# Fourteen blocks of the first feed-forward matrix quantised during attention, diagonal tiles regrouped, low-rank closers issued by four

## The chip, the cores and the metric

The kernel runs on the 8 cores of one Trainium2 chip. Each core computes one of the 8 sequences of the batch; the weights are the same for all, and the cores exchange nothing. The metric is the device time in microseconds of the slowest core.

## What is computed

```
x = layernorm(x + attention(x) @ W_O)              # 2048 tokens, 1024 features, 16 heads of 64 + 32 rotary
    Q = [cq @ W_UQ, rope(cq @ W_QR)], K = [ckv @ W_UK, rope(x @ W_KR)], V = ckv @ W_UV
    scores = clip(Q K^T, -80, 80), causal, softmax(scores / sqrt(96)) @ V
x = layernorm(x + W_proj'(gelu(W_fc' x)))           # 1024 -> 4096 -> 1024
    W' x = fake_quant(W) x + b + 2 * B (A x)        # low-rank adapter of rank 16
    fake_quant(W): s = max|W| / 127;  round(W / s) clipped to [-128, 127], times s
```

The scale s is one number for each matrix, so the whole matrix must have been read once before any of it can be rounded.

## The kernel before

All five engines run programs written out by hand, with semaphores between them; each engine does its work in the order in which the program lists it. Four stretches follow one another.

**Inputs.** Up to about 91 us the latent projections, the values (into the tile VP, all in bf16) and the first pair of heads are made.

**Attention.** Heads go in 8 pairs (NPAIR). A pair has 36 units (NU), numbered g = 0 to 287 over the pairs. A unit is one tile of 128 keys against a block of 512 queries, for both heads of the pair. In a query block the three tiles past the first diagonal one (kt = 4 qb + 1, + 2, + 3, of 384, 256 and 128 columns) share two units. For each unit TensorE writes scores into one of two PSUM slots (PSD0, PSD1; `scores`, L551), ScalarE takes the exponential into one of eight tiles PT0 to PT7 (L802), VectorE clips it (L1036 on the diagonal, L1040 elsewhere), and five units later (LAG) TensorE multiplies by the values (L582) and by ones for the denominators (L588). `released` holds back the scores of item j until the slot of item j - 2 was read. Four "next" items in each pair make the queries and keys of the next pair (L563), copied out by ScalarE (L810) and VectorE (L1022). A "scale" item spreads the quantisation scales to all partitions.

Beside this both feed-forward matrices are read once, 64 blocks of 512 KB, and VectorE takes the maximum of one block every fourth unit (`absmax`, L946, up to g = 253). The scales follow at g = 262 and 266, and from g = 274 VectorE rounds 7 pieces (`round_piece`, L881).

**Output projection and first layer norm.** TensorE does 32 steps s, each 8 matmuls with W_O (L659) and two sums over the features (`sums`, L632, L635). VectorE adds the residual (L1064), subtracts the mean (`centred`, L996) and multiplies by the inverse deviation (`normal`, L1001). ScalarE makes a copy and a square (L834, L835). The first matrix is quantised in these steps: ScalarE adds the magic number that rounds (L820), VectorE subtracts it and writes bf16 (`integers`, L889). Pieces are numbered k = 0 to 63, of which 0 to 31 are the first matrix (RTF) and 32 to 63 the second (RTP). SyncE loads them (L437) into 15 buffers (STG, QX and, when their tokens are normalised, the residual tiles XR).

**Feed-forward.** Eight chunks t of 256 tokens. `up(t, oc)` makes block oc of 32: 8 matmuls with RTF (L703) and a closer (L711), the low-rank part, which for t = 0 has 16 rows and for later t 128 rows, most of them zero. UPB gives five PSUM banks in turn. ScalarE applies gelu (L856). `down(t, dc)` is 32 matmuls with RTP (L724), then the adapter (L729), and `statistics` of the second layer norm (L679, L682), which need the sum that VectorE makes (L1136). In chunk 0 VectorE still quantises: `quant_upto(dc)` says up to which piece before the sum of block dc.

## Time and profile before

| | |
|---|---|
| three runs | 1077.07, 1077.62 and 1115.05 us, median 1077.62 |
| profiled execution | 1077.04 us, span of its slowest core (core 6) 1075.4 us |
| spans of the eight cores | 1071.1 to 1075.4 us |
| TensorE busy | 976.9 us, 91% of the span |
| ScalarE busy | 658.0 us, 61% |
| VectorE busy | 546.3 us, 51% |
| GpSimd busy | 60.1 us, 6% |

The span reaches from the first to the last instruction of a core. A busy share is a mean over all stretches: ScalarE and VectorE work hardest in attention, and little in the feed-forward part. Engine times of matmuls are modelled and may overlap by a little. The run of 1115.05 us lies apart from the other two, which are within 0.05%.

### The profile page before, as it was taken

What the parts mean: (1) busy time and instruction counts of PE and PEld (TensorE: products, weight loads), DVE (VectorE), ACT (ScalarE), POOL (GpSimd) and SP (SyncE); (2) the same over time, 40 slices, a digit from 0 to 9 for tenths busy, and PEclk for the clock granted to TensorE, in tenths of its full rate; (3) what the DMA queues carried; (4) which work ended last, traced back from release to release, by engine and by line L of the source; (5) the groups of instructions that cost most, each with busy time, mean ns of one, the idle gap of its engine ahead of it and who ended that gap; (6) DMA issues with size and microseconds to landing.
All of it is one profiled execution on the core that took longest, in us unless ns stands there. A gap on an engine that the chain in (4) does not pass through costs nothing.

```text
span 1075.4 us, 23227 instructions; the slowest of 8 cores (1071.1 to 1075.4 us)
## 1 busy us (share of the span) xinstructions
PE 976.9 (91%) x8227; PEld 668.5 (62%) x8242; DVE 546.3 (51%) x1059; ACT 658.0 (61%) x954; POOL 60.1 (6%) x113
## 2 busy tenths in 40 slices
PE   4998888888898888997789999999999999999995
PEld 1343444444444444443356788888888888888884
DVE  4457787887878877779895403112031120402114
...
GB/s 132 176 85 41 117 109 127 100 128 99 148 145 131 128 71 279 223 259 219 170 183 208 68 1 18 24 7 35 2 26 16 16 26 1 41 1 21 21 12 69
DMA packets 35439, 99.05 MB, mean 92 GB/s; under 512 B 4544, under 2 KB 12992, under 8 KB 34944
## 3 DMA queue, kind: packets, MB, share of 16 engines
...
## 4 chain that ended last, share of the span: by engine, by line
PE 66%; ACT 10%; DVE 10%; issue 8%; DMA 5%; POOL 1%; DVEq 0%; ACTq 0%; SPq 0%; POOLq 0%
PE PSD L703 17%; PE PS L724 15%; PE PSD L551 8%; ACT PT L802 7%; PE PSD L724 5%; PE PS L703 4%; DMA WUK<-wUK 4%; DVE QK L1022 2%; PE PSD L711 2%; PE PSD L563 2%; ACT RD L770 2%; PE BIG L582 2%; PE BIG L588 2%; DVE XA L1001 1%; PE PS L582 1%
## 5 line engine op out<-in xcount | busy, mean ns | idle before, releaser
L802 ACT ACTIVATE PT<-PSD 128x1024 bf16<-128x1024 f32 (+1 forms) x288 | 271.4, 979 | 21.8 <-PE PSD L551 20.0
L703 PE MATMUL PSD<-XA,RTF 128*128 128x256 bf16 x1664 | 212.8, 276 | 5.4 <-ACT HH L856 3.1
L551 PE MATMUL PSD<-QK 96*64 96x512 bf16 (+7 forms) x1280 | 175.9, 356 | 33.3 <-ACT PT L802 18.6
L703 PEld LDWEIGHTS PSD<-XA,RTF 128*128 128x128 bf16 x1664 | 162.2, 99 | 28.7 <-issue 6.7
L724 PE MATMUL PS<-HH,RTP 128*128 128x256 bf16 x1536 | 176.6, 274 | 0.0
L856 ACT ACTIVATE HH<-PSD,BFCS,SML 128x256 bf16<-128x256 f32 x208 | 115.0, 564 | 81.2 <-PE PSD L711 80.8
L724 PEld LDWEIGHTS PS<-HH,RTP 128*128 128x128 bf16 x1536 | 149.8, 98 | 19.8 <-issue 1.7
L551 PEld LDWEIGHTS PSD<-QK 96*64 96x64 bf16 (+1 forms) x1280 | 63.5, 109 | 125.4 <-issue 114.8
L1040 DVE TENSOR_SCALAR PT<-PT 128x1024 bf16<-128x1024 bf16 (+3 forms) x288 | 108.4, 381 | 42.0 <-ACT PT L802 39.7
L1125 DVE TENSOR_SCALAR UPt<-PSD,SML 128x256 bf16<-128x256 f32 x8 | 3.9, 484 | 234.2 <-PE PSD L743 234.2
L1136 DVE TENSOR_TENSOR XA<-PTMP,XA 128x256 bf16<-128x256 f32 x64 | 27.2, 425 | 143.8 <-ACT PTMP L865 143.6
L865 ACT ACTIVATE PTMP<-PS,BPRS,SML 128x256 f32<-128x256 f32 x48 | 26.9, 561 | 111.8 <-PE PS L729 111.8
L946 DVE TENSOR_REDUCE MXW<-STG 128x1 f32<-128x1024 f32 x64 | 77.7, 1214 | 0.0
L582 PE MATMUL BIG<-PT,VP 128*64 128x512 bf16 (+3 forms) x384 | 70.0, 351 | 4.1 <-DVE XA L952 3.7
L588 PE MATMUL BIG<-PT,ONES 128*64 128x512 bf16 (+3 forms) x384 | 70.1, 351 | 0.0
L659 PE MATMUL PSD<-XA,WOB 128*128 128x512 bf16 x249 | 59.6, 379 | 0.5 <-issue 0.2
L871 ACT ACTIVATE TSQ<-XA 128x256 bf16<-128x256 bf16 x64 | 26.7, 417 | 54.3 <-DVE XA L1136 54.3
L724 PE MATMUL PSD<-HH,RTP 128*128 128x256 bf16 x512 | 58.5, 273 | 0.0
L1036 DVE SCALAR_TENSOR_TENSOR PT<-PT,TRI 128x256 bf16<-128x256 bf16 (+1 forms) x96 | 48.9, 510 | 15.4 <-ACT PT L802 14.7
L724 PEld LDWEIGHTS PSD<-HH,RTP 128*128 128x128 bf16 x512 | 50.1, 98 | 5.8
L703 PE MATMUL PS<-XA,RTF 128*128 128x256 bf16 x384 | 49.8, 273 | 0.0
L711 PE MATMUL PSD<-UZ,BSF 128*128 128x256 bf16 x182 | 49.6, 273 | 0.0
...
## 6 DMA issues: line engine op xcount, KB each, us to landing
STG<-wFCr POOLq DMA_DIRECT2D x32, 512.0 KB, 3.9
STG<-wPRr POOLq DMA_DIRECT2D x32, 512.0 KB, 4.1
STG<-wPRr SPq DMA_DIRECT2D x24, 512.0 KB, 5.1
STG<-wFCr SPq DMA_DIRECT2D x20, 512.0 KB, 8.6
XR<-xP POOLq DMA_DIRECT2D x16, 512.0 KB, 8.6
...
QX<-wFCr SPq DMA_DIRECT2D x12, 512.0 KB, 8.7
XR<-wPRr SPq DMA_DIRECT2D x8, 512.0 KB, 7.6
```

Of the source, the lines that this page charges most:

```text
L551: mm = e.matmul(PSD[slot][64 * hf:64 * hf + 64, 512 * i + at:512 * i + at + ext], KH[c % 2][i][0:rows, 128 * kt + 64 * hf:128 * kt + 64 * ...
L582: e.matmul(OB[n % 2][64 * i:64 * i + 64, lq:lq + ext], VP[:, o:o + 64], PTB[g % NPT][:, 512 * i + at:512 * i + at + ext], start=first, sto ...
L588: mm = e.matmul(DB[n % 2][64 * i:64 * i + 64, lq:lq + ext], ONES[:, :], PTB[g % NPT][:, 512 * i + at:512 * i + at + ext], start=first, sto ...
L659: mm = e.matmul(BK[s % 4][:, 0:512], WOB[:, 1024 * ds + 128 * hc:1024 * ds + 128 * hc + 128], xa(hc, 512 * nb, 512), start=(hc == 0), stop ...
L703: e.matmul(UPB[oc % 5][:, 0:TC], RTF[:, 1024 * oc + 128 * i:1024 * oc + 128 * i + 128], xa(i, TC * t, TC), start=(i == 0), stop=False)
L711: e.matmul(UPB[oc % 5][:, 0:TC], lhs, rhs, start=False, stop=True).then_inc(s_fc, 1)
L724: e.matmul(DNB[dc % 3][:, 0:TC], RTP[dc][:, 128 * f:128 * f + 128], HH[:, TC * f:TC * f + TC], start=(f == 0), stop=False)
L802: e.activation(heads2(PTB[a % NPT], 0, ext), heads2(PSD[j % 2], 0, ext), AF.Exp, scale=ISQ).then_inc(s_exp, 1)
L856: e.activation(HH[:, TC * oc:TC * oc + TC], UPB[oc % 5][:, 0:TC], AF.Gelu, bias=BFCS[:, oc:oc + 1], scale=SML[:, 2:3]).then_inc(s_gelu, 1)
L946: e.tensor_reduce(MXW[:, ci:ci + 1], STG[:, 1024 * (ci % 4):1024 * (ci % 4) + 1024], AXX, ALU.max, apply_absolute_value=True).then_inc(s_a ...
L1036: e.scalar_tensor_tensor(heads2(pt, 0, lo), heads2(pt, 0, lo), LO, TRI[:, 0:2 * lo].rearrange("p (h x) -> p h x", h=2), ALU.max, ALU.min). ...
L1040: e.tensor_scalar(heads2(pt, lo, ext), heads2(pt, lo, ext), HI, LO, ALU.min, ALU.max).then_inc(s_clip, 1)
```

## The change

1. 14 pieces (EARLY) are quantised during attention. Piece k is rounded by VectorE at unit g = 181 + 7k and subtracted at g = 184 + 7k, so up to g = 275. They pass through the three QX buffers. Their output is written into blocks 8 to 21 of RTF (BLOCKS), which is where the values VP lie. VP is laid out by pairs of heads now, 2048 columns a pair, so that a pair's values are free when its attention is done: `integers(k)` waits for s_pv = 36 (k // 2 + 1).
2. The two scales are no longer made together. The maximum of the first matrix is taken at g = 132 and its scale at g = 140, with a second "scale" item behind unit 148.
3. SyncE issues the loads of pieces 0 to 6 behind the queries of pair 6 (when the scores of 180 units are done) and of 7 to 13 behind those of pair 7.
4. In the output projection ScalarE's rounding and VectorE's subtraction are in steps 3 to 20 and 4 to 21 as before, but VectorE has none in steps 15, 16 and 17 and none after 21. ScalarE's last two pieces, behind the last deviation, are gone. VectorE rounds pieces 36 to 45 itself. `quant_upto` is 58 + 3 dc in place of 56 + 3 dc, and there are 19 buffers, four of them in XR0.
5. The units of the diagonal are 384 and 128 + 256 columns in place of 128 + 384 and 256.
6. For chunk 0 the closers of four blocks stand together behind the fourth block, each with 32 rows in a strip of its own.

```diff
@@ pair_units
-        units += [(qb, [4 * qb + 3, 4 * qb + 1]), (qb, [4 * qb + 2])]
+        units += [(qb, [4 * qb + 1]), (qb, [4 * qb + 3, 4 * qb + 2])]
...
-SCALE_AT = NG - 26
+SCALE_AT = (140, NG - 26)
...
+    EARLY, EARLY_AT = 14, 181
+    BLOCKS = list(range(8, 22)) + list(range(8)) + list(range(22, 32))
...
-    BUF = [k % 7 for k in range(32)] + [7, 8, 9, 10, 0, 1, 2, 3, 11, 12, 13, 14] + \
-        [k % 4 for k in range(44, NK)]
+    BUF = [4 + k % 3 for k in range(EARLY)] + [k % 7 for k in range(EARLY, 32)] + \
+        [0, 1, 2, 3, 0, 1, 9, 10, 2, 3, 11, 12, 13, 14, 0, 1, 2, 3, 15, 16, 17, 18] + \
+        [k % 4 for k in range(54, NK)]
+    RESIDUAL = {9: 16, 11: 24, 15: 32}
-    ON_SCALAR = range(7, 38)
+    ON_SCALAR = range(21, 36)
...
-        return min(NK, 56 + 3 * dc)
+        return min(NK, 58 + 3 * dc)
@@ sp
         for c in range(1, NPAIR - 1):
             e.wait_ge(s_qk, NU * c)
             rotary(c + 1)
+            if c == 3:
+                maximum(0)
+            if c == 5:
+                for k in range(7):
+                    fetch(k)
+        for k in range(7, EARLY):
+            fetch(k)
+        maximum(1)
@@ pe, attend
-                    o = D * kt + 64 * (2 * c + i)
+                    o = 2048 * c + 128 * kt + 64 * i
@@ pe, up
-            else:
-                rows = slice(32 * r, 32 * r + 16)
-                lhs, rhs = BSF[rows, 128 * q:128 * q + 128], UO[rows, o:o + TC]
-            e.matmul(UPB[oc % 5][:, 0:TC], lhs, rhs, start=False, stop=True).then_inc(s_fc, 1)
+            elif r == 3:
+                for j in range(4):
+                    rows = slice(32 * j, 32 * j + 32)
+                    e.matmul(UPB[(oc - 3 + j) % 5][:, 0:TC], BSF[rows, 128 * q:128 * q + 128],
+                             UO[rows, 0:TC], start=False, stop=True).then_inc(s_fc, 1)
@@ act
-            if s >= 3:
-                round_piece(s + 4)
+            if 3 <= s < 14:
+                round_piece(s + 18)
+            elif 17 <= s < 21:
+                round_piece(s + 15)
         deviation(3)
-        round_piece(36)
-        round_piece(37)
@@ dve
+            k = (g - EARLY_AT) // 7
+            if 0 <= k < EARLY and (g - EARLY_AT) % 7 == 0:
+                if k == 0:
+                    e.wait_ge(s_sml, 1)
+                round_piece(k)
+            if 0 <= k < EARLY and (g - EARLY_AT) % 7 == 3:
+                e.wait_ge(s_pv, NU * (k // 2 + 1))
+                integers(k)
...
-            elif s >= 4:
-                integers(s + 3)
+            elif 4 <= s < 15:
+                integers(s + 17)
+            elif 18 <= s < 22:
+                integers(s + 14)
...
-        integers(35)
         for md in (6, 7):
             normal(2, md)
         moments(3)
-        integers(36)
-        for k in range(38, 45):
+        round_piece(36)
+        for k in range(37, 46):
             quant_step(k)
```

VectorE in attention, units 180 (PT4) to 184 (PT0) before. L1036 and L1040 clip, L946 is the maximum, L1022 copies out the keys and queries of the next pair:

```order
L1036 SCALAR_TENSOR_TENSOR PT4_66<-PT4_66,TRI_74 128x2x128
L1040 TENSOR_SCALAR PT4_66<-PT4_66 128x2x384
L1036 SCALAR_TENSOR_TENSOR PT5_67<-PT5_67,TRI_74 128x2x256
L1040 TENSOR_SCALAR PT5_67<-PT5_67 128x2x256
L946 TENSOR_REDUCE MXW_126<-STG_72 128x1
L1036 SCALAR_TENSOR_TENSOR PT6_68<-PT6_68,TRI_74 128x2x128
L1040 TENSOR_SCALAR PT6_68<-PT6_68 128x2x128
L1040 TENSOR_SCALAR PT7_69<-PT7_69 128x1024
L1040 TENSOR_SCALAR PT0_62<-PT0_62 128x1024
L1022 CAST QK0_59<-PSD0 64x2x512
```

The same stretch in the changed kernel, where L1066, L1070, L975 and L1051 are those lines, L910 rounds and L918 subtracts:

```order
L1066 SCALAR_TENSOR_TENSOR PT4_66<-PT4_66,TRI_74 128x2x128
L1070 TENSOR_SCALAR PT4_66<-PT4_66 128x2x384
L1066 SCALAR_TENSOR_TENSOR PT5_67<-PT5_67,TRI_74 128x2x128
L1070 TENSOR_SCALAR PT5_67<-PT5_67 128x2x256
L975 TENSOR_REDUCE MXW_126<-STG_72 128x1
L910 TENSOR_SCALAR QX0_76<-QX0_76,SML_130 128x1024
L1066 SCALAR_TENSOR_TENSOR PT6_68<-PT6_68,TRI_74 128x2x256
L1070 TENSOR_SCALAR PT6_68<-PT6_68 128x2x128
L1070 TENSOR_SCALAR PT7_69<-PT7_69 128x1024
L1070 TENSOR_SCALAR PT0_62<-PT0_62 128x1024
L918 TENSOR_SCALAR RTF_86<-QX0_76 128x1024
L1051 CAST QK0_59<-PSD1 64x2x512
```

Piece 0 is rounded behind unit 181's maximum and subtracted just ahead of the copy for the next pair; the two diagonal units have changed shapes.

VectorE in the output projection, steps 15, 16 and 17 before (L1064 adds, L996 subtracts the mean, L889 subtracts the magic number, L1001 normalises, L984 begins the moments of the second quarter):

```order
L1064 TENSOR_TENSOR XR1_80<-PSD1,XR1_80 128x512
L996 TENSOR_TENSOR XR0_79<-XR0_79,PS4 128x512 x2
L889 TENSOR_SCALAR RTF_86<-QX0_76 128x1024
L1001 TENSOR_TENSOR XA_43<-XR0_79,RSC0_99 128x512 x2
L1064 TENSOR_TENSOR XR2_81<-PSD0,XR2_81 128x512
L996 TENSOR_TENSOR XR0_79<-XR0_79,PS4 128x512 x2
L889 TENSOR_SCALAR RTF_86<-QX1_77 128x1024
L1001 TENSOR_TENSOR XA_43<-XR0_79,RSC0_99 128x512 x2
L1064 TENSOR_TENSOR XR2_81<-PSD0,XR2_81 128x512
L889 TENSOR_SCALAR RTF_86<-QX2_78 128x1024
L984 COPY RSC1_100<-BIG 128x512
```

The same steps in the changed kernel (L1100, L1025, L1030 and L1013 are L1064, L996, L1001 and L984):

```order
L1100 TENSOR_TENSOR XR1_80<-PSD1,XR1_80 128x512
L1025 TENSOR_TENSOR XR0_79<-XR0_79,PS4 128x512 x2
L1030 TENSOR_TENSOR XA_43<-XR0_79,RSC0_99 128x512 x2
L1100 TENSOR_TENSOR XR2_81<-PSD0,XR2_81 128x512
L1025 TENSOR_TENSOR XR0_79<-XR0_79,PS4 128x512 x2
L1030 TENSOR_TENSOR XA_43<-XR0_79,RSC0_99 128x512 x2
L1100 TENSOR_TENSOR XR2_81<-PSD0,XR2_81 128x512
L1013 COPY RSC1_100<-BIG 128x512
```

The three L889 are gone from these steps.

TensorE at the start of chunk 0 before, blocks 0 to 3 (L703 the matmuls, L711 the closer):

```order
L703 MATMUL PSD0<-XA_43,RTF_86 128x256 x8
L711 MATMUL PSD0<-UO_106,BSF_84 128x256
L703 MATMUL PSD1<-XA_43,RTF_86 128x256 x8
L711 MATMUL PSD1<-UO_106,BSF_84 128x256
L703 MATMUL PSD1<-XA_43,RTF_86 128x256 x8
L711 MATMUL PSD1<-UO_106,BSF_84 128x256
L703 MATMUL PSD0<-XA_43,RTF_86 128x256 x8
L711 MATMUL PSD0<-UO_106,BSF_84 128x256
```

In the changed kernel (L728 and L738), blocks 0 to 4:

```order
L728 MATMUL PSD0<-XA_43,RTF_86 128x256 x8
L728 MATMUL PSD1<-XA_43,RTF_86 128x256 x16
L728 MATMUL PSD0<-XA_43,RTF_86 128x256 x8
L738 MATMUL PSD0<-UO_106,BSF_84 128x256
L738 MATMUL PSD1<-UO_106,BSF_84 128x256 x2
L738 MATMUL PSD0<-UO_106,BSF_84 128x256
L728 MATMUL PS4<-XA_43,RTF_86 128x256 x8
```

The four closers now follow block 3, each into its own bank.

## Rows read from the trace of the kernel before

**Rows 1.** Busy time by stretch; columns: stretch, length, PE, PEld, DVE, ACT, POOL, clock, DMA share, GB/s

```profile
540.00:580.00 40.00, 37.95 (x271) 25.14 (x272) 30.07 (x48) 18.91 (x34) 0.00 (x0) 0.91 0.64 200
580.00:600.00 20.00, 15.17 (x144) 11.80 (x143) 13.34 (x22) 2.83 (x6) 0.00 (x0) 0.91 0.55 185
```

**Rows 2.** The same view, one pair of heads in attention

```profile
314.80:358.40 43.60, 37.98 (x354) 19.62 (x350) 35.00 (x66) 40.40 (x48) 7.08 (x13) 1.00 0.53 139
```

**Rows 3.** Timeline of ACT beside small units; start us, us, engine, line, instruction, idle before

```profile
341.31 0.60 ACT L802 ACTIVATE PT<-PSD 128x512 bf16<-128x512 f32 x1 [0.38 <-PE PSD L551]
...
405.69 1.94 ACT L802 ACTIVATE PT<-PSD 128x1024 bf16<-128x1024 f32 x2 [0.43 <-PE PSD L551]
```

**Rows 4.** Timeline of ACT behind the "scale" item

```profile
424.32 1.51 ACT L802 ACTIVATE PT<-PSD 128x1024 bf16<-128x1024 f32 x2 [0.93 <-PE PSD L551]
```

**Rows 5.** Timeline of DVE, rounding and subtracting one piece after another

```profile
541.53 0.69 DVE L889 TENSOR_SCALAR RTP<-STG 128x1024 bf16<-128x1024 f32 x1
542.13 0.75 DVE L881 TENSOR_SCALAR XR<-XR,SML 128x1024 f32<-128x1024 f32 x1
542.80 0.69 DVE L889 TENSOR_SCALAR RTP<-STG 128x1024 bf16<-128x1024 f32 x1
```

**Rows 6.** Timeline of DVE at the end of the output projection

```profile
523.78 0.69 DVE L1001 TENSOR_TENSOR XA<-XR,RSC 128x512 bf16<-128x512 f32 x1
524.38 0.69 DVE L1064 TENSOR_TENSOR XR<-PSD,XR 128x512 f32<-128x512 f32 x1
...
526.78 0.69 DVE L1064 TENSOR_TENSOR XR<-PSD,XR 128x512 f32<-128x512 f32 x1
...
530.37 0.76 DVE L1007 TENSOR_SCALAR UO<-PS,SML 128x512 bf16<-128x512 f32 x1
```

**Rows 7.** Timeline of ACT between output projection and first gelu

```profile
536.41 0.63 ACT L776 ACTIVATE RSC<-RSC 128x512 f32<-128x512 f32 x1 [6.52 <-DVE RSC L988]
...
537.67 2.36 ACT L820 ACTIVATE STG<-STG,MAGC,SML 128x1024 f32<-128x1024 f32 x2
540.05 1.28 ACT L856 ACT_TABLE_LOAD   x1
541.34 1.93 ACT L856 ACTIVATE HH<-PSD,BFCS,SML 128x256 bf16<-128x256 f32 x4
```

**Rows 8.** Timeline of PE from the last two output projection steps into chunk 0

```profile
521.52 1.89 PE L659 MATMUL PSD<-XA,WOB 128*128 128x512 bf16 x8
...
523.68 1.89 PE L659 MATMUL PSD<-XA,WOB 128*128 128x512 bf16 x8
...
531.57 1.87 PE L703 MATMUL PSD<-XA,RTF 128*128 128x256 bf16 x8 [2.29 <-DVE UO L1007]
...
542.05 1.87 PE L703 MATMUL PSD<-XA,RTF 128*128 128x256 bf16 x8 [3.10 <-ACT HH L856]
...
549.58 1.05 PE L703 MATMUL PS<-XA,RTF 128*128 128x256 bf16 x8
550.55 0.28 PE L711 MATMUL PS<-UO,BSF 16*128 16x256 bf16 x1
550.76 1.05 PE L703 MATMUL PSD<-XA,RTF 128*128 128x256 bf16 x8
...
576.94 3.67 PE L724 MATMUL PS<-HH,RTP 128*128 128x256 bf16 x32
...
593.06 0.37 PE L679 MATMUL BIG<-XA,ONEM 128*128 128x256 bf16 x1 [3.93 <-DVE XA L1136]
```

**Rows 9.** Timeline of DVE in chunk 0, pieces 48, 53 and 59

```profile
563.16 0.75 DVE L881 TENSOR_SCALAR STG<-STG,SML 128x1024 f32<-128x1024 f32 x1 [1.21 <-DMA STG<-wPRr]
...
573.50 0.75 DVE L881 TENSOR_SCALAR STG<-STG,SML 128x1024 f32<-128x1024 f32 x1 [0.19 <-DMA STG<-wPRr]
...
591.23 0.75 DVE L881 TENSOR_SCALAR STG<-STG,SML 128x1024 f32<-128x1024 f32 x1
```

**Rows 10.** The page's DMA issues; source and target, count, KB, median us from issue to landing

```profile
STG<-wPRr SPq DMA_DIRECT2D x24, 512.0 KB, 5.1
```

More of the change, by code:

```diff
@@ L107, in score_items @@
                 items.append(("next", c + 1, NEXT_AT.index(u)))
-            if NU * c + u == SCALE_AT + 8:
-                items.append(("scale", 0, 0))
+            for m in range(2):
+                if NU * c + u == SCALE_AT[m] + 8:
+                    items.append(("scale", m, 0))
     return items
@@ L276, in build @@
     s_y = sem("s_y")
-    d_qw = [sem("d_qw%d" % i) for i in range(15)]
+    d_qw = [sem("d_qw%d" % i) for i in range(19)]
     s_q1 = sem("s_q1")
@@ L395, in released @@
         else:
-            e.wait_ge(s_sml, 1)
+            e.wait_ge(s_sml, a + 1)
     def heads2(t, a, b):
@@ L424, in sp, with maximum, fetch @@
         rotary(1)
+        def maximum(m):
+            e.wait_ge(s_mxr, m + 1)
+            e.dma_start(MXT[0:1, 128 * m:128 * m + 128], MXR[:, m:m + 1]).then_inc(d_mx, 16)
+        def fetch(k):
+            if USE[k] > 1:
+                e.wait_ge(s_q2, k - BUF[:k][::-1].index(BUF[k]))
+            if BUF[k] in RESIDUAL:
+                e.wait_ge(s_xt, RESIDUAL[BUF[k]])
+            e.dma_start(slot_of(k), piece(k)[0]).then_inc(d_qw[BUF[k]], 16)
         for c in range(1, NPAIR - 1):
@@ L427, in sp @@
             rotary(c + 1)
-        e.wait_ge(s_mxr, 2)
-        e.dma_start(MXT[0:1, 0:256], MXR[:, 0:2]).then_inc(d_mx, 16)
-        e.wait_ge(s_ax, 64)
-        for k in range(NK):
-            if USE[k] > 1:
-                e.wait_ge(s_q2, k - BUF[:k][::-1].index(BUF[k]))
-            if BUF[k] in (7, 11):
-                e.wait_ge(s_xt, 16 if BUF[k] == 7 else 24)
-            e.dma_start(slot_of(k), piece(k)[0]).then_inc(d_qw[BUF[k]], 16)
+            if c == 3:
[6 more added lines that the diff above has]
+        maximum(1)
+        e.wait_ge(s_ax, 64)
+        for k in range(EARLY, NK):
+            fetch(k)
         for n in range(8 * NTC):
@@ L580, in attend @@
                 for i in range(2):
-                    o = D * kt + 64 * (2 * c + i)
+                    o = 2048 * c + 128 * kt + 64 * i
                     e.matmul(OB[n % 2][64 * i:64 * i + 64, lq:lq + ext], VP[:, o:o + 64],
                              PTB[g % NPT][:, 512 * i + at:512 * i + at + ext],
-                             start=first, stop=last)
+                             start=first, stop=last and kt == kts[-1])
             for kt, qlo, ext, at in parts(u):
@@ L589, in attend @@
                                   PTB[g % NPT][:, 512 * i + at:512 * i + at + ext],
-                                  start=first, stop=last)
+                                  start=first, stop=last and kt == kts[-1])
             mm.then_inc(s_pv, 1)
@@ L614, in pe @@
             else:
-                e.wait_ge(s_mx1, 16)
-                e.matmul(PSD[j % 2][:, 0:6], ONERF[0:1, :], MX1[0:1, 32:38], start=True,
-                         stop=True).then_inc(s_smm, 1)
+                e.wait_ge(s_mx1, 8 * a + 8)
+                e.matmul(PSD[j % 2][:, 0:3], ONERF[0:1, :], MX1[0:1, 32 + 3 * a:35 + 3 * a],
+                         start=True, stop=True).then_inc(s_smm, 1)
         for g in range(NG - LAG, NG):
@@ L706, in up @@
             if t:
-                lhs, rhs = BSF[:, 128 * q:128 * q + 128], UZ[r][:, o:o + TC]
-            else:
-                rows = slice(32 * r, 32 * r + 16)
-                lhs, rhs = BSF[rows, 128 * q:128 * q + 128], UO[rows, o:o + TC]
-            e.matmul(UPB[oc % 5][:, 0:TC], lhs, rhs, start=False, stop=True).then_inc(s_fc, 1)
+                e.matmul(UPB[oc % 5][:, 0:TC], BSF[:, 128 * q:128 * q + 128], UZ[r][:, o:o + TC],
+                         start=False, stop=True).then_inc(s_fc, 1)
+            elif r == 3:
[3 more added lines that the diff above has]
+                             UO[rows, 0:TC], start=False, stop=True).then_inc(s_fc, 1)
         def down(t, dc):
@@ L789, in act @@
             elif kind == "v":
-                o = D * (4 * nb + m // 2) + 512 * (m % 2)
-                e.copy(VP[:, o:o + 512], bank[:, 0:512]).then_inc(s_eva, 1)
+                e.copy(VP[:, :].rearrange("p (c k x) -> p c k x", c=8, k=16)[
+                    :, 4 * (m % 2):4 * (m % 2) + 4, 4 * nb + m // 2, :],
+                    bank[:, 0:512].rearrange("p (c x) -> p c x", c=4)).then_inc(s_eva, 1)
             elif kind == "pq":
@@ L1043, in dve @@
                 absmax(g // 4)
-            if g == SCALE_AT - 8:
-                e.wait_ge(s_ax, 64)
-                for m in range(2):
-                    e.tensor_reduce(MXR[:, m:m + 1], MXW[:, 32 * m:32 * m + 32], AXX,
-                                    ALU.max).then_inc(s_mxr, 1)
-            if g in (SCALE_AT, SCALE_AT + 4):
-                scale((g - SCALE_AT) // 4)
-            if SCALE_AT + 12 <= g and g % 2 == 0:
-                if g == SCALE_AT + 12:
-                    e.wait_ge(s_sml, 1)
-                round_piece((g - SCALE_AT - 12) // 2)
+            if g + 8 in SCALE_AT:
+                m = SCALE_AT.index(g + 8)
+                e.wait_ge(s_ax, 32 * m + 32)
+                e.tensor_reduce(MXR[:, m:m + 1], MXW[:, 32 * m:32 * m + 32], AXX,
+                                ALU.max).then_inc(s_mxr, 1)
+            if g in SCALE_AT:
+                scale(SCALE_AT.index(g))
+            k = (g - EARLY_AT) // 7
+            if 0 <= k < EARLY and (g - EARLY_AT) % 7 == 0:
+                if k == 0:
+                    e.wait_ge(s_sml, 1)
+                round_piece(k)
+            if 0 <= k < EARLY and (g - EARLY_AT) % 7 == 3:
+                e.wait_ge(s_pv, NU * (k // 2 + 1))
+                integers(k)
+            if g >= NG - 14 and g % 2 == 0:
+                round_piece(EARLY + (g - NG + 14) // 2)
         normalise(4 * NPAIR - 1)
```

25 lines of the change are left out of this document (14 added, 11 removed).

## The prediction

> **What bounds the kernel now.** I read the busy times by stretch first, then the timelines of the engines where TensorE sits idle, then the loads. From 600 us on the matmuls of the feed-forward part follow each other without a break, and the change touches none of them. What can move lies in three places.
>
> In attention a pair of heads takes 43.6 us [rows 2]. ScalarE is busy for 40.4 of them, TensorE for 38.0, VectorE for 35.0, so VectorE has 8.6 us to spare in a pair. The limit is ScalarE with the two PSUM slots: the exponential of unit j cannot start before the scores of j, and these wait until the exponential of j - 2 is done. Beside a unit of 256 columns ScalarE idles, because its own work is short (0.60 us against 1.02) and the next scores are not there: 0.38 us once a pair and 0.43 us twice a pair, the first row and the kind of the second in [rows 3].
>
> In the output projection a step of 10 matmuls takes TensorE 2.16 us (521.52 to 523.68 [rows 8]). VectorE starts a row every 0.60 us [rows 6] and has four in an ordinary step (add, centre, subtract the magic number, normalise), so 2.4 us: it, and not TensorE, sets the pace from about step 13. After the last step TensorE waits for VectorE's UO (2.29 us) and, five blocks later, for the first gelu (3.10 us) [rows 8]. That gelu waits in ScalarE's row behind the deviation, two roundings and the table load [rows 7].
>
> In chunk 0 a block of `up` takes 1.19 us, of which the 8 matmuls are 0.87 (three rows of [rows 8], 549.58 to 550.76: 0.97 to the closer, 0.21 to the next block). In `down`, VectorE is in line behind pieces that SyncE has not loaded, and TensorE waits 3.93 us for its sum (the row at 593.06). The granted clock is 0.91 in both stretches from 540 to 600 us [rows 1], because TensorE falls back to 1.2 GHz after these waits.
>
> **Attention, part by part.** The two diagonal units keep their 768 columns. Only the split changes: exponentials of about 0.81 us each (midway between 0.60 and 1.02) in place of 1.02 and 0.60. The scores two units behind the first of them are released 0.21 us earlier. Four diagonals a pair and 8 pairs give 6.7 us. Bounds: nothing, if another chain comes last there, and 8 x (0.38 + 0.43 + 0.43) = 9.9 us if all of that idle time goes. I take 6.7, because the waiting row is ScalarE's on the path in every case of [rows 3].
>
> The second "scale" item takes a slot and brings no attention work. The one of before shows 0.93 us of idle ScalarE behind it [rows 4]: + 0.9.
>
> Rounding and subtracting a piece cost VectorE 0.67 and 0.60 us from start to start [rows 5], 17.8 us for 14. In a pair these are 5 pieces, 6.4 us, against the 8.6 us to spare [rows 2], and after g = 253 the maxima are gone. So most of it is hidden. What is not: VectorE also serves the copies for the next pair and the normalisation, on which TensorE waits, and behind the subtraction of pieces 4 to 13 these come up to 0.6 us later. I count some four such places, + 2 (between 0, all hidden, and + 8, when a late copy costs 0.7 us in each of 11 cases). Piece 0 is the special case: its load is issued when the scores of unit 179 are done, and VectorE wants it two units later, some 5 us on with the maximum ahead of it. Two loads of queries go out first, and a load of this size lands 5.1 us after issue [rows 10]. VectorE then stands for 1 to 2 us, and the clips behind it have some 2.5 us before TensorE, five units later, needs them: + 1 (0 to 4). Pieces 1 to 13 are issued over ten units ahead. SyncE has the queries of pair 7 behind piece 6, which waits for the subtraction at g = 205; they are free to go at g = 216 anyway. Attention in all: - 6.7 + 0.9 + 2 + 1 = **- 2.8 us**, between - 9 and + 6.
>
> **Output projection to the first gelu.** Up to step 14 every piece has its step as before, so nothing changes. In steps 15 to 17 and 22 to 25 the 7 subtractions go, 7 x 0.60 = 4.2 us, and the last step of TensorE starts 4.2 us earlier (519.5 instead of 523.7). It can't be more, since from step 26 VectorE is ahead and the adapter and three steps of TensorE follow the moments. Now VectorE's last addition follows TensorE's step at once, where it started 3.1 us behind its start at 523.68 [rows 6, 8]; it would start when these matmuls end, 1.9 us behind, 1.2 us gained. One subtraction less before UO is 0.6. UO comes 4.2 + 1.2 + 0.6 = 6.0 us earlier, and `up` starts at 525.6. The moments behind it lose one more subtraction, 6.6 us. ScalarE's two roundings (2.36 us [rows 7]) are gone. The first gelu is 9.0 us earlier, at 532.3. TensorE has done blocks 0 to 4 by about 531.8, so the wait is still there but falls from 3.1 to about 1.3 us, and block 5 starts at 533.1 instead of 542.05: **- 9.0 us**.
>
> **The rest of `up` in chunk 0.** Before, 27 blocks took 34.9 us (542.05 to 576.94): 27 x 1.19 = 32.1, and 2.8 for the low clock behind the wait. Now 27 x 0.87 = 23.5. A closer costs 0.10 us of gap, 0.11 itself and 0.11 of gap again. Nothing in this trace shows four closers in a row, each on 32 rows of its own. One after another they would take 0.65 us, all at once 0.32, and with a gap around each 1.28, which is no gain. I take 0.5: 7 x 0.5 = 3.5 us. For the low clock 1.4 us (0 to 2.8). One new wait: gelu 28 and 29 can only start behind the last four closers, and `down` asks for gelu 29. With 1.93 us for four gelus [rows 7], two and the way to them are 1.35 us, where block 29 was long done. In all 29.8 us: **- 5.1 us**, and `down` starts at 562.8.
>
> The Trainium skill, page "TensorEngine Tiling (Array Packing)", section "Key Properties", says that tiles of 32 rows by 128 columns work in parallel, and that a change of tiling mode drains the array. The 0.1 us on either side of the closer agrees with the second; no row here shows the first. By that page four closers would cost 0.32 us, and the term would be 1.3 us better.
>
> **`down` in chunk 0.** TensorE no longer decides, the loads do. VectorE ends its moments 6.6 us earlier, at 529.7 (the deviation at 536.41 [rows 7] waits for them), and does one rounding and 9 pairs (12.1 us), then 16 rows of centring and normalising at 0.60 (9.6 us): 551.4. Only then is XR0 free for piece 50, which lands at about 556.5 [rows 10]. Behind the sum of block 1 now stand pieces up to 61, where they were up to 59. Before, pieces 48 to 53 came 2.07 us apart (563.16 to 573.50 [rows 9]). At that rate piece 61 lands at 579.3, and the statistics follow 1.83 us behind the rounding (591.23 to 593.06 [rows 8, 9]): 581.1, 12.0 us earlier than before. The other bound: eight buffers are free at once instead of four; were TensorE the limit, the statistics came at 575, 18 us earlier. I take a rate a little better than before, 579.6: **- 13.5 us at this point**, so 0.6 of the 14.1 is given back. From here the rest is as before.
>
> **Sum.** - 13.5 - 2.8 = - 16.3 us, from the profiled execution's 1077.04 (span 1075.4 and 1.6 around it) 1060.7. The median shown is 0.6 above that execution, so 1061.3; I say **1061**. That is 1.5%, within the 2% (21.6 us, to 1056.1) that a measurement of this kernel can about tell from no change.
>
> **Rivals.** (a) More goes: the closers run at once (- 1.3), the clock doesn't fall (- 1.4), loads keep up (- 3) and the diagonal gives 8 (- 1.3): 1054. For it speaks that four closers use different rows and banks; against it that it wants several things together. 0.22. (b) The loads decide in full: pieces of the second matrix keep the 2.07 us spacing or fall to the 2.8 us that 185 GB/s in [rows 1] would mean for 512 KB; piece 61 comes up to 8 us later than the first bound, and a closer keeps its own gap. 8 us are lost of the 13.5, less if only one holds: 1065 to 1069. For it speaks that TensorE waits on just these loads today. 0.2. (c) VectorE becomes the bound of attention: it decides if the 6.4 us a pair and its waits for TensorE and ScalarE together exceed the 8.6 us to spare, for then each piece pushes clips, copies and so TensorE. All 17.8 us exposed and the diagonal without gain: 1077.6 - 13.5 + 0.9 + 17.8 = 1083, slower than before. Against it speak [rows 2] and the end of the maxima at g = 253. 0.04. (d) The change doesn't do what it says in attention, the idle time beside small units only moves: 1067. 0.04.
>
> **Numbers.** The forecast, 1056 to 1065, has 0.5. With (a) and (b) taken in, the range is 1052 to 1070. Faster by over 2% is (a) and a little of the forecast's edge, 0.25; slower by over 2% needs more than (c), 0.02; within, 0.73.
>
> **What would show it.** Right: pairs 1 to 4 at 42.8 us in place of 43.6 and pairs 5 and 6 near 43.5; `up` starting 82 us behind the first step of the projection, where it was 88; blocks of chunk 0 at 1.0 us on average; a TensorE wait of 3 to 5 us at the second statistics. Wrong: VectorE over 97% busy in pairs 5 and 6 with TensorE waiting for L1070 or L1051; closers 0.3 us each; no wait at the statistics, or one over 8 us.

## The result, and the profile after

| | before | after |
|---|---|---|
| median | 1077.34 us (4 runs, 1076.81 to 1115.05) | 1069.97 us (4 runs, 1068.53 to 1071.93) |
| ratio after / before | | 0.9934, interval 0.9913 to 0.9955 |
| profiled execution, span | 1077.04, 1075.4 us (core 6) | 1071.93, 1070.4 us (core 7) |
| spans of the cores | 1071.1 to 1075.4 us | 1060.2 to 1070.4 us |

In some executions, that of 1115.05 us among them, the cores of one die or of both run at a lower granted clock, and all ratios and intervals here leave these out.

The change brings 7.1 us by the ratio, 0.7%, where 16.3 were forecast. The cores now differ by 10 us, where they differed by 4. The table shows where. Each number is the distance between the starts of two rows in the timelines, read on all eight cores.

| stretch | before | after | forecast |
|---|---|---|---|
| pairs 1 to 3, each | 43.63 | 43.44 | 42.8 |
| pair 4 (second scale item) | 43.63 | 44.52 (45.66 on core 4) | 43.7 |
| pair 5 (piece 0) | 43.91 | 45.2 to 49.0 | about 43.5, and 1 for piece 0 |
| pair 6 | 43.75 | 44.8, 46.0 on two cores | near 43.5 |
| first exponential to first step with W_O | 347.1 to 348.2 | 349.6 to 355.9 | 2.8 less |
| that step to the first matmul of `up` | 88.0 | 82.0 | 82.0 |
| `up` to `down`, chunk 0 | 42.6 to 45.4 | 34.9 to 36.6 | 37.2 |
| `down` to its second statistics | 15.7 to 16.5 | 15.5 to 17.8 | 16.8 |
| from there to the end | 482.4 to 483.5 | 481.5 to 483.0 | unchanged |

Behind attention only `down` came above its forecast, by up to 1.0 us on five cores. From the start of `up` to the second statistics, 54.0 us in the forecast, seven cores took 51.7 to 53.2 and core 7 took 54.3. Attention grew by 1.7 us (core 3) to 7.8 us (core 4), 4.7 on the mean of the cores.

**Attention.** The timelines of core 7, in which L910 rounds, L1051 copies queries and keys and L981 normalises, first VectorE:

```profile
319.32 1.21 DVE L975 TENSOR_REDUCE MXW<-STG 128x1 f32<-128x1024 f32 x1
321.72 0.75 DVE L910 TENSOR_SCALAR QX<-QX,SML 128x1024 f32<-128x1024 f32 x1 [1.18 <-DMA QX<-wFCr]
...
323.79 0.69 DVE L918 TENSOR_SCALAR RTF<-QX 128x1024 bf16<-128x1024 f32 x1
324.51 1.23 DVE L1051 CAST QK<-PSD 64x1024 bf16<-64x1024 f32 x1
```

and TensorE beside it:

```profile
323.55 0.35 PE L613 MATMUL PS<-PT,ONES 128*64 128x384 bf16 x2
325.88 0.62 PE L575 MATMUL PSD<-QK 96*64 96x512 bf16 x4 [1.98 <-DVE QK L1051]
...
328.30 0.64 PE L607 MATMUL BIG<-PT,VP 128*64 128x512 bf16 x2 [1.13 <-DVE XA L981]
...
330.62 1.09 PE L575 MATMUL PSD<-QK 96*64 96x512 bf16 x4
```

VectorE stands 1.18 us for piece 0, whose load is not there. The copy for the next pair comes late, and TensorE waits 1.98 us for it and 1.13 us for the normalisation. Then four matmuls that took 0.62 us take 1.09. The windows of core 7 (the last columns are granted clock, DMA share, GB/s) show the clock beside it:

```profile
322.00:326.00 4.00, 2.02 (x20) 0.99 (x18) 3.94 (x8) 3.11 (x4) 0.00 (x0) 1.00 0.95 227
326.00:330.00 4.00, 2.87 (x30) 1.90 (x29) 3.97 (x9) 2.73 (x4) 1.23 (x2) 0.65 1.08 288
330.00:334.00 4.00, 4.00 (x21) 1.89 (x18) 3.22 (x6) 1.98 (x3) 0.42 (x1) 0.50 0.97 281
334.00:338.00 4.00, 3.34 (x31) 1.74 (x29) 2.68 (x4) 3.66 (x4) 0.11 (x1) 1.00 0.64 177
```

TensorE is busy for 2.0 of 4 us, and then its clock falls to 0.50, the 1.2 GHz level, and comes back. Six of eight cores show such a fall in pair 5. On the two that don't, 1 and 3, the pair takes 45.4 and 45.2 us, on the others 47.0 to 49.0. The clock falls once more in pair 4 on core 4 and in pair 6 on cores 4 and 7; these are the 45.66 and the 46.0 us of the table.

One wait of ScalarE stands in each of the other pairs, here behind the "next" item at unit 18:

```profile
165.25 1.01 ACT L839 CAST QK<-PSD 64x1024 bf16<-64x1024 f32 x1 [0.26 <-PE PSD L587]
166.16 0.80 ACT L831 ACTIVATE PT<-PSD 128x768 bf16<-128x768 f32 x1
167.70 1.89 ACT L831 ACTIVATE PT<-PSD 128x768 bf16<-128x768 f32 x2 [0.74 <-PE PSD L575]
```

and the row of TensorE that it waits for:

```profile
167.03 0.52 PE L575 MATMUL PSD<-QK 96*64 96x128 bf16 x8 [0.67 <-DVE QK L1051]
```

The waits of [rows 3] beside small units are gone, but unit 20 now waits until VectorE, which has a maximum and the copy of 1.23 us to do, has read the slot that it needs. Its row at 167.70 is unit 20, with 0.74 us of idle ScalarE.

**Projection to `down`.** TensorE again, core 7; these answer to [rows 8]:

```profile
527.25 1.89 PE L684 MATMUL PSD<-XA,WOB 128*128 128x512 bf16 x8
533.44 3.65 PE L728 MATMUL PSD<-XA,RTF 128*128 128x256 bf16 x32 [1.69 <-DVE UO L1036]
...
541.06 4.19 PE L728 MATMUL PSD<-XA,RTF 128*128 128x256 bf16 x24 [2.76 <-ACT HH L885]
...
547.32 1.91 PE L728 MATMUL PSD<-XA,RTF 128*128 128x256 bf16 x16
549.16 0.28 PE L738 MATMUL PSD<-UO,BSF 32*128 32x256 bf16 x1
549.16 0.28 PE L738 MATMUL PS<-UO,BSF 32*128 32x256 bf16 x1
549.17 0.28 PE L738 MATMUL PSD<-UO,BSF 32*128 32x256 bf16 x2
549.38 1.92 PE L728 MATMUL PSD<-XA,RTF 128*128 128x256 bf16 x16
...
569.91 3.65 PE L752 MATMUL PS<-HH,RTP 128*128 128x256 bf16 x32 [1.36 <-ACT HH L885]
...
587.73 0.37 PE L704 MATMUL BIG<-XA,ONEM 128*128 128x256 bf16 x1 [5.64 <-DVE XA L1173]
```

`up` starts 6.2 us behind the last projection step (533.44 - 527.25), where it took 7.9. The closers of one group start within 0.01 us of each other, and the next matmul 0.22 us later. The wait for the first gelu is 2.76 us, that for the sum 5.64 (1.1 to 2.8 and 3.4 to 5.6 over the cores). Two rows of VectorE (pieces of the second matrix) show what is behind the latter:

```profile
577.89 0.75 DVE L910 TENSOR_SCALAR STG<-STG,SML 128x1024 f32<-128x1024 f32 x1 [1.15 <-DMA STG<-wPRr]
...
584.62 0.75 DVE L910 TENSOR_SCALAR STG<-STG,SML 128x1024 f32<-128x1024 f32 x1 [1.64 <-DMA STG<-wPRr]
```

### The profile page after: what moved, and what is told of

It reads as the page before. It is cut to its first block, busy times and chain, and to the rows that moved or that the text cites. A ratio compares the mean times of both kernels' runs of the same rounds, so it can differ in the third digit from the quotient of the medians.

```text
span 1070.4 us, 23266 instructions; the slowest of 8 cores (1060.2 to 1070.4 us)
## 1 busy us (share of the span) xinstructions
PE 970.2 (91%) x8244; PEld 669.2 (63%) x8244; DVE 556.0 (52%) x1076; ACT 640.2 (60%) x938; POOL 61.8 (6%) x113
## 3 DMA queue, kind: packets, MB, share of 16 engines
q1 hardware_dynamic: 19968, 44.60, 13.4%
## 4 chain that ended last, share of the span: by engine, by line
PE 60%; DVE 12%; ACT 11%; issue 9%; DMA 6%; POOL 1%; DVEq 0%; ACTq 0%; SPq 0%; POOLq 0%
PE PS L752 15%; PE PSD L728 15%; ACT PT L831 8%; PE PSD L575 7%; PE PSD L752 5%; DMA WUK<-wUK 4%; PE PS L728 3%; DVE QK L1051 3%; PE PSD L587 2%; PE PSD L732 2%; DMA STG<-wPRr 2%; ACT RD L798 1%; DVE XA L1030 1%; DVE XR L1100 1%; PE PS L613 1%
## 5 line engine op out<-in xcount | busy, mean ns | idle before, releaser
L728 PE MATMUL PSD<-XA,RTF 128*128 128x256 bf16 x1664 | 207.8, 274 | 4.4 <-ACT HH L885 2.8
L575 PE MATMUL PSD<-QK 96*64 96x512 bf16 (+7 forms) x1280 | 178.1, 359 | 36.3 <-ACT PT L831 15.4
L728 PEld LDWEIGHTS PSD<-XA,RTF 128*128 128x128 bf16 x1664 | 162.7, 98 | 25.1 <-issue 5.2
L1070 DVE TENSOR_SCALAR PT<-PT 128x1024 bf16<-128x1024 bf16 (+3 forms) x288 | 107.1, 378 | 33.9 <-ACT PT L831 32.0
L975 DVE TENSOR_REDUCE MXW<-STG 128x1 f32<-128x1024 f32 x64 | 77.5, 1212 | 0.0
L1066 DVE SCALAR_TENSOR_TENSOR PT<-PT,TRI 128x256 bf16<-128x256 bf16 (+1 forms) x96 | 48.9, 509 | 12.8 <-ACT PT L831 12.2
L728 PE MATMUL PS<-XA,RTF 128*128 128x256 bf16 x384 | 49.8, 273 | 0.0
```

The lines of the kernel that those rows point to most:

```text
L575: mm = e.matmul(PSD[slot][64 * hf:64 * hf + 64, 512 * i + at:512 * i + at + ext], KH[c % 2][i][0:rows, 128 * kt + 64 * hf:128 * kt + 64 * ...
L728: e.matmul(UPB[oc % 5][:, 0:TC], RTF[:, 1024 * oc + 128 * i:1024 * oc + 128 * i + 128], xa(i, TC * t, TC), start=(i == 0), stop=False)
L975: e.tensor_reduce(MXW[:, ci:ci + 1], STG[:, 1024 * (ci % 4):1024 * (ci % 4) + 1024], AXX, ALU.max, apply_absolute_value=True).then_inc(s_a ...
L1066: e.scalar_tensor_tensor(heads2(pt, 0, lo), heads2(pt, 0, lo), LO, TRI[:, 0:2 * lo].rearrange("p (h x) -> p h x", h=2), ALU.max, ALU.min). ...
L1070: e.tensor_scalar(heads2(pt, lo, ext), heads2(pt, lo, ext), HI, LO, ALU.min, ALU.max).then_inc(s_clip, 1)
```

## The experiments

Two theories stood for the lost microseconds in attention. **A**: piece 0's late load, and the low clock behind it, cost most of it. **B**: VectorE's own work for the 14 pieces costs it. Beside them **C**: the new split's gain is eaten by the copy behind the item at unit 18. **D**: in `down` the sum of a block stands behind more pieces than the loads can bring. **E**: the faster `up` is given back in `down`. Pair times hold for all cores unless said.

**1. Load early.** The changed kernel, with pieces 0 to 2 loaded one pair sooner.

```diff
+            if c == 4:
+                for k in range(3):
+                    fetch(k)
             if c == 5:
-                for k in range(7):
+                for k in range(3, 7):
                     fetch(k)
```

> The changed kernel, but SyncE issues the first three early pieces one pair of heads sooner (behind the scores of unit 143, not 179). In the changed kernel VectorE waits 1.0 to 2.4 us for the load of piece 0 at the start of pair 5, TensorE then waits 1.8 to 2.0 us for the copy and 1.1 us for the normalisation, and on six cores its clock falls to half for 4 to 8 us. Theory A (this one landing starts it, and the lost clock multiplies it): pair 5 falls from 45.2 to 49.0 us on the cores to some 44.0 to 44.5 on all of them, the cores come within 3 us of each other, and the slowest ends 4 to 5 us earlier, near 1065. Theory B (VectorE has too much to do in pair 5, the load is incidental): pair 5 stays over 45 us on most cores and the time within 1.5 us of 1070.

Measured: 1066.38 us, ratio to before 0.9909 (0.9894 to 0.9925), 3.6 us less than the changed kernel, or 2.7 by the two ratios. Pair 5 took 44.32 us on four cores and 45.68 on the other four. VectorE no longer waits for the load. TensorE, core 7:

```profile
321.22 0.62 PE L578 MATMUL PSD<-QK 96*64 96x512 bf16 x4 [0.70 <-DVE QK L1054]
323.64 0.41 PE L610 MATMUL BIG<-PT,VP 128*64 128x512 bf16 x2 [1.13 <-DVE XA L984]
```

The first wait fell from 1.98 to 0.70 us, the second stays at 1.13. All eight cores show these two waits within 0.02 us, and yet the clock fell on 0, 1, 4 and 6, to 0.61 to 0.71 in the worst 4 us, and not on the others. (In pair 6 it fell on core 2, which took 45.99 us there.) A is right in part: on the mean of the cores pair 5 went from 47.2 to 45.0 us, and from 49.0 to 45.7 on the slowest. It is not the whole loss, as experiment 2 shows. Of what attention won, 1.0 us on the mean was given back in `down`, which took 16.3 to 20.0 us to its second statistics.

**2. One column.** Experiment 1, with the 28 early rows of VectorE working on one column instead of 1024. These 14 blocks of RTF are left out of the result and filled with zeros by GpSimd in the output projection, so only attention is to be read. The cut shows the main lines.

```diff
-                round_piece(k)
+                e.tensor_scalar(slot_of(k)[:, 0:1], slot_of(k)[:, 0:1], SML[:, 0:1], MAGIC, ...)
-                integers(k)
+                e.tensor_scalar(slot_of(k)[:, 0:1], slot_of(k)[:, 0:1], MAGIC, None, ...)
@@ pool
+        for b in range(8, 22):
+            e.memset(RTF[:, 1024 * b:1024 * b + 1024], 0.0)
```

> As load_early, but the 28 rows with which VectorE rounds and subtracts the 14 pieces in attention work on one column instead of 1024, and the 14 blocks are filled with zeros by GpSimd during the output projection; so these blocks of the first matrix are left out of the result. Loads, waits and order stay. Theory A: with the load early, VectorE's 17.8 us cost only 2 us or so in all, so attention is 1 to 3 us shorter than in load_early. Theory B (VectorE's work is what attention pays for): pairs 5 and 6 come down to 43.4 us each, as pairs 1 to 3 have, which is 4 us or more below load_early.

Measured: pair 5 43.73 us and pair 6 43.51, against 44.32 or 45.68 and 44.82 (45.99 on core 2). So VectorE's work costs 0.6 us (1.95 where the clock fell) in pair 5 and 1.3 (2.5 on core 2) in pair 6, 1.9 to 3.3 in all and 2.7 on the mean; 2 was forecast. B is right in part as well: on the mean of the cores VectorE's work costs a little more than the late load, 2.7 against 2.2 us, while on the slowest core the load costs more. The median of the whole kernel, 1091.11 us, is not to be compared; the last section says what is known of it.

**3. Next item moved.** Experiment 1, with the third "next" item behind unit 23.

```diff
-NEXT_AT = (5, 12, 18, 29)
+NEXT_AT = (5, 12, 23, 29)
```

> As load_early, and the third item for the next pair stands behind unit 23 of a pair instead of 18. In the changed kernel ScalarE idles 0.74 us once a pair just behind that item, before the second of the two diagonal units 19 and 20, which used to be 0.38 and 0.27 us; a pair of heads is 0.19 us shorter than before and not 0.84 as forecast. Theory C (VectorE's copy for the next pair, which takes 1.23 us, holds the slot that unit 20 needs, and unit 20 is now the longer one): the 0.74 us go, and pairs 1 to 3 fall from 43.44 to about 43.0 us or less, 3 us over the eight pairs. Rival (the 0.21 us a diagonal was never on the path, TensorE's own row is): pairs stay within 0.1 us of 43.44.

Measured: 1063.93 us, ratio 0.9887 (0.9871 to 0.9903). Pair 1 takes 43.17 us, pairs 2 and 3 43.06, pair 4 44.14, pairs 5 and 6 44.60 and 44.54. ScalarE in the same part of a pair, core 7 (L842 is the copy of the next item, behind unit 23):

```profile
189.21 1.00 ACT L842 CAST QK<-PSD 64x1024 bf16<-64x1024 f32 x1
190.10 2.16 ACT L834 ACTIVATE PT<-PSD 128x1024 bf16<-128x1024 f32 x2
192.63 0.82 ACT L834 ACTIVATE PT<-PSD 128x768 bf16<-128x768 f32 x1
...
193.84 3.68 ACT L834 ACTIVATE PT<-PSD 128x768 bf16<-128x768 f32 x4
```

The wait of 0.74 us is gone. 0.27 us of it is won in pair 1, 0.38 in pairs 2 to 4 and 0.28 in pair 6; pair 5 is 0.28 us longer than on the cores of experiment 1 that kept their clock, and 1.1 shorter than on the others. C is right. Pairs 2 and 3 are now 0.57 us shorter than before, of the 0.84 forecast. Where the other 0.27 went is not shown.

**4. Diagonal only.** Before, with the new split alone.

```diff
-        units += [(qb, [4 * qb + 3, 4 * qb + 1]), (qb, [4 * qb + 2])]
+        units += [(qb, [4 * qb + 1]), (qb, [4 * qb + 3, 4 * qb + 2])]
```

> The kernel before with nothing but the new split of the diagonal units. If the split is worth what pairs 1 to 3 of the changed kernel show, 0.19 us a pair, the whole is 1.5 us faster than before. My forecast was 0.84 us a pair, 6.7 us.

Measured: 1076.05 us, ratio 0.9989 (0.9965 to 1.0014). Pairs take 43.44 us. ScalarE, core 7, same place as above:

```profile
162.18 1.01 ACT L811 CAST QK<-PSD 64x1024 bf16<-64x1024 f32 x1 [0.26 <-PE PSD L563]
163.09 0.80 ACT L803 ACTIVATE PT<-PSD 128x768 bf16<-128x768 f32 x1
164.63 5.78 ACT L803 ACTIVATE PT<-PSD 128x768 bf16<-128x768 f32 x6 [0.74 <-PE PSD L551]
```

The pattern and its 0.74 us are those of the changed kernel, without any of its other parts. 0.19 us a pair in pairs 1 to 5, 0.15 in pair 6 and 0.6 in the last one: attention is 1.6 us shorter on the mean of the cores, where the prediction had 6.7.

**5. Before with the next item moved.** Does the item at unit 18 hurt without the new split too?

```diff
-NEXT_AT = (5, 12, 18, 29)
+NEXT_AT = (5, 12, 23, 29)
```

> The kernel before with the third item for the next pair behind unit 23 in place of 18 and nothing else. By theory C the item behind unit 18 also cost the old split something, 0.38 and 0.27 us of idle ScalarE a pair, but less than the new one: pairs of about 43.2 in place of 43.63, 2 to 3 us in all, 1074 to 1075. If it stays at 1077, the item hurt only the new split.

Measured: 1077.56 us, ratio 1.001 (0.9999 to 1.002); pairs 2 to 4 take 43.51 for 43.63 us, pairs 1 and 5 43.79 for 43.63 and 43.91, pair 6 43.51 for 43.75. So the item at unit 18 cost the old split 0.12 us in most pairs and the new one 0.38: the item and the new split hinder each other. With the item moved in both, the split is worth 43.51 - 43.06 = 0.45 us in pairs 2 and 3.

**6. Second scale item only.** Before, with the two scales made apart as in the change.

```diff
-SCALE_AT = NG - 26
+SCALE_AT = (140, NG - 26)
```

> The kernel before with the two scales made at their new places, that is with a second scale item behind unit 148, and nothing else. Pair 4 was 43.63 us and is 44.52 in the changed kernel and in one_column: the item alone should bring it to 44.7, and the whole to 1.0 us slower. If pair 4 stays at 43.6, the 1 us belongs to something else of the change.

Measured: 1076.40 us, ratio 1.0 (0.999 to 1.0011). Pair 4 takes 44.30 us, 0.67 more than before. With the new split it takes 1.08 more than pair 3 (44.52 and 43.44). The forecast of 0.9 lies between. The whole kernel does not show it: 0.7 us is within the interval of the ratio.

**7. Closers only.** Before, with the closers by four; the closer behind each single block goes.

```diff
+            elif r == 3:
+                for j in range(4):
+                    rows = slice(32 * j, 32 * j + 32)
+                    e.matmul(UPB[(oc - 3 + j) % 5][:, 0:TC], BSF[rows, ...], UO[rows, 0:TC], ...)
```

> The kernel before with the closers of chunk 0 by four and nothing else. In the changed kernel four closers take 0.32 us more than the matmuls (0.28 us of rows beside each other, and 0.1 to either side), as if at once. If that is all, up to down of chunk 0 falls from 44.2 or 45.4 us by 8 x 1.0 less 1.4 for the new wait for gelu 29, 6.6 us, but the sum of block 1 comes when the loads and VectorE have it ready, so TensorE waits longer there and of the 6.6 us little is left: 1 us or less at the end (theory E). The rival, that nothing is behind it, gives 1070.5.

Measured: 1074.67 us, ratio 0.998 (0.997 to 0.9991). `up` to `down` took 37.8 to 40.5 us for 42.6 to 45.4, but `down` to the second statistics 16.6 to 19.2 for 15.7 to 16.5. On the mean of the cores 4.1 us were won up to `down` and 1.3 of them given back by the second statistics; the ratio says 2.2 us for the whole. TensorE, core 3, the slowest:

```profile
571.94 3.65 PE L726 MATMUL PS<-HH,RTP 128*128 128x256 bf16 x32 [1.36 <-DVE RTP L891]
...
588.72 0.37 PE L679 MATMUL BIG<-XA,ONEM 128*128 128x256 bf16 x1 [4.62 <-DVE XA L1138]
...
597.36 0.27 PE L679 MATMUL BIG<-XA,ONEM 128*128 128x256 bf16 x1 [2.86 <-DVE XA L1138]
```

The wait at the second statistics, 3.6 to 4.3 us over the cores before (3.93 in [rows 8]), is 4.4 to 5.9 here, 4.62 on this core. The wait of 2.86 at the third is this core's alone; the others have 1.0 or less. E holds in part.

**8. Before with two pieces between sums.** VectorE makes the sum of block dc when it has rounded piece 56 + 2 dc, and not 56 + 3 dc.

```diff
-        return min(NK, 56 + 3 * dc)
+        return min(NK, 56 + 2 * dc)
```

> The kernel before with quant_upto 56 + 2 dc in place of 56 + 3 dc and nothing else. By theory D the 3.9 us wait of TensorE for the sum of block 1, and about 1 us of low clock, go here too: about 1073. By the rival the time stays at 1077.

Measured: 1072.13 us, ratio 0.9955 (0.9938 to 0.9973). `down` to the second statistics took 12.6 us on six cores and 12.8 on two, 3 to 4 us less than before, and the third statistics come about 5 us sooner. TensorE, core 4:

```profile
587.30 0.27 PE L679 MATMUL BIG<-XA,ONEM 128*128 128x256 bf16 x1 [0.38 <-DVE XA L1136]
592.73 0.27 PE L679 MATMUL BIG<-XA,ONEM 128*128 128x256 bf16 x1 [0.91 <-DVE XA L1136]
```

The wait at the second statistics is 0.38 us now (0.7 on two cores), where it was 3.6 to 4.3, and the sum of block 1 is not held up by loads. D is right, in the kernel before too.

**9. The changed kernel with two pieces between sums.** The same line, where the changed kernel has 58 + 3 dc.

> The changed kernel with quant_upto 56 + 2 dc and nothing else. By theory D the first down to the second statistics takes 12.55 us on every core in place of 15.5 to 17.8, and the time is 4 to 5.5 us below 1070, near 1065. The rest of the kernel, pair 5 with its 45 to 49 us too, stays.

Measured: 1061.34 to 1063.37 us in three executions, ratio to before 0.9869 (0.9849 to 0.9889). `down` to the second statistics took 12.55 us on six cores, 12.80 and 12.85 on two, for 15.5 to 17.8. Pair 5 took 46.1 to 48.8 us, with a fall of the clock on all eight cores. The time is 7 to 9 us below the changed kernel's, where 4 to 5.5 were expected. The stretch from `down` on gives 3 to 5 us. The rest lies in part in attention, which took 353.7 us on its slowest core where it had taken 355.9, and no core's clock fell in pair 4 or 6; this edit touches nothing there, so I take it for chance.

**10. Later loads.** The changed kernel with pieces 0 to 6 loaded two units later still.

```diff
             if c == 5:
+                e.wait_ge(s_qk, NU * c + 2)
                 for k in range(7):
                     fetch(k)
```

> The changed kernel with the loads of pieces 0 to 6 issued two units later still (behind the scores of unit 181). Theory A (landing of piece 0, then the clock): VectorE waits about 2 us longer, 3 to 4.5 us, TensorE's clock falls on all eight cores, pair 5 lasts 49 to 51 us on every core and the time is 1072 to 1074, 2 to 4 us above the changed kernel. Theory B (VectorE's amount of work): pair 5 and the time as in the changed kernel, within 1 us.

Measured: 1070.44 us, ratio 0.9943 (0.9927 to 0.9959), less than A expected. VectorE waited 1.2 to 2.5 us for piece 0 (median of the cores 2.0), where it had waited 0.8 to 2.5 (median 1.5), so about half a microsecond was added and not two units. The clock fell on all eight cores, and pair 5 took 46.6 to 49.0 us, on cores 1 and 3 48.0 and 47.7 (45.4 and 45.2 in the changed kernel). VectorE, core 0:

```profile
322.06 0.76 DVE L911 TENSOR_SCALAR QX<-QX,SML 128x1024 f32<-128x1024 f32 x1 [2.42 <-DMA QX<-wFCr]
```

TensorE and the windows behind it:

```profile
326.23 0.62 PE L576 MATMUL PSD<-QK 96*64 96x512 bf16 x4 [3.23 <-DVE QK L1052]
...
326.00:330.00 4.00, 3.10 (x28) 1.90 (x30) 3.94 (x10) 2.73 (x4) 1.22 (x2) 0.61 1.01 307
330.00:334.00 4.00, 4.00 (x25) 2.13 (x23) 3.57 (x6) 1.84 (x2) 0.07 (x1) 0.53 0.91 264
```

This run settles nothing for A or B. SyncE was still busy with the queries of pair 6, so the load of piece 0 went out only 0.4 us later (0.69 us behind the first exponential of pair 5, for 0.28). And in experiment 9, where these loads stand as in the changed kernel, the clock fell on all eight cores too, and cores 1 and 3 took 47.95 and 47.30 us. What shows A is experiment 1.

**11. All three mended.** Experiment 3 (loads early, item moved) with two pieces between sums.

> As next_moved, and quant_upto is 56 + 2 dc in place of 58 + 3 dc: two pieces instead of three stand ahead of VectorE's sum of each block in chunk 0, and the sum of block 1 is behind piece 58, not 61. TensorE waited 5.6 us there in the changed kernel, and the first 32 matmuls behind the wait ran at the low clock (6.0 us instead of 3.7). Theory D (the order of VectorE's row makes this wait; the loads would be in time for the matmuls that need them): the wait and the low clock go, first down to second statistics falls from 17 to 19 us to about 12.5, and the time by 5 to 8 us, to 1056 to 1059. Rival (the loads decide: TensorE waits as long, only later, for the rounded pieces of blocks 6 and 7): the time stays within 1.5 us of next_moved's 1063.9.

Measured: 1058.55 us (1057.59 to 1060.13), ratio 0.9836 (0.9817 to 0.9855), about 18 us less than before and 11 less than the change as it was. It is the fastest kernel here. On no core did the clock fall in pair 5, the pair took 44.6 us everywhere, as in experiment 3, and TensorE's waits at the second and third statistics are, on core 7:

```profile
573.96 0.27 PE L707 MATMUL BIG<-XA,ONEM 128*128 128x256 bf16 x1 [0.38 <-DVE XA L1176]
579.48 0.27 PE L707 MATMUL BIG<-XA,ONEM 128*128 128x256 bf16 x1 [1.00 <-DVE XA L1176]
```

while VectorE still waits for loads in between, 1.90 us for one, where nobody waits for VectorE:

```profile
577.64 0.76 DVE L913 TENSOR_SCALAR STG<-STG,SML 128x1024 f32<-128x1024 f32 x1 [1.90 <-DMA STG<-wPRr]
```

## Why the prediction was wrong in attention and right behind it

The time is at the upper end of the range, but the forecast of - 16.3 us had one sum wrong: "Attention in all: - 6.7 + 0.9 + 2 + 1 = - 2.8 us". It came out at + 1.7 to + 7.8, by core. Its four parts, measured each:

- **Diagonal, - 6.7: wrong in mechanism and size, - 1.6.** Experiments 4 and 3. The step "the waiting row is ScalarE's on the path in every case of [rows 3]" counted what the old wait cost, and not which wait comes last once it is gone. The "next" item at unit 18 holds a slot until VectorE has copied it (1.23 us, behind a maximum of 1.21), and unit 20 needs the slot. In the old split the same item cost 0.12 us in most pairs (experiment 5), in the new one 0.38. The copy explains only that much; with the item moved, a pair is still 0.27 us short of the forecast, and that part is open. The rival (d), that the idle time only moves, had just this mechanism, and was given 0.04. It gave 1067; its own terms, 1077.6 - 13.5 + 3.9, make 1068.
- **Second scale item, + 0.9: right.** 0.67 alone, 1.08 with the new split, and 2.2 on core 4, where the clock fell behind it.
- **VectorE's work, + 2: right.** 1.9 to 3.3, and in pair 5 the waits are those for the copy (0.70 us) and the normalisation (1.13), as counted.
- **Landing of piece 0, + 1 (0 to 4): the cause was seen and the size wrong.** By experiment 1 it cost 0.9 us on the cores that kept their clock and up to 4.7 on the others (45.2 and 49.0 against 44.32). The prediction had VectorE standing for 1 to 2 us, and it stood for 0.8 to 2.5; the prediction then let 2.5 us of slack in the clips absorb it. The clips were not what was short. The copy for the next pair was, with the subtraction of piece 0 just ahead of it, and the normalisation behind. The term also had no clock in it, though the same kind of wait was priced with one in chunk 0.

On core 3, whose clock held, the parts add up to - 1.6 + 1.1 + 1.9 + 0.9 = + 2.3 us, against 1.7 seen. On core 4 they are - 1.6 + 2.2 + 1.9 + 4.7, and 1.2 more for a fall of the clock in pair 6, together + 8.4, against 7.8 seen. Pair 0, which no part of this sum concerns but the split, was 0.35 and 0.6 us shorter there than before, which is about the difference.

**Output projection to `up`, - 6.0: right** to 0.1 us, 82.0 for 88.0. The first gelu came 6.9 us behind the start of `up` (540.35 on core 7), where 6.7 was forecast. The wait for it was 2.76 us on core 7 and not 1.3, since the five blocks ahead of it were done 4.9 us behind the start of `up` (537.25 + 1.05 in the timeline), and not 6.2; five blocks at the 1.19 us of before are 5.95. On five cores the wait was 1.1 to 1.4 us, but for another reason: their clock fell ahead of these blocks (core 1: the first 32 matmuls take 4.97 us for 3.65), and block 5 starts 7.6 us behind `up` on all eight.

**Rest of `up`, - 5.1: right in sign and a little small.** From block 5 to `down` 28.85 us (core 7) against 34.9 (core 6), so - 6.0. What I had left open between 0.32 and 1.28 us for four closers is 0.32: four blocks take 3.82 us (549.38 to 553.20 in the timeline), 8 matmuls of a block 0.875. The Trainium skill says in "TensorEngine Tiling (Array Packing)", "Key Properties", that different tiles can run matmuls in parallel, and the trace agrees: four closers start within 0.01 us and take 0.28. The 0.5 I took was too cautious. The wait for gelu 29 was forecast at 1.35 us and is 1.36.

**`down`, 0.6 given back: right**, 15.5 to 17.8 us against 16.8 forecast, with a wait of 3.4 to 5.6 us where 3 to 5 was said. The reason was right as well, pieces that are not loaded. But the loads don't have to cause it: it comes from the order of VectorE's list, as experiments 8 and 9 show.

Rival (c), VectorE as the bound of attention, gave 1083 and did not come: VectorE was over 97% busy for a few microseconds in pair 5 (3.94 and 3.97 of 4 in the windows above), but not through the pair (41.2 of 47.7 us on core 7, 41.05 of 45.2 on core 3). Why the clock falls on some cores and not on others with the same waits is open (experiments 1, 3 and 11).
